# A decoder layer on one core: the last two groups' Toeplitz convolutions as fp32r products of high and low parts

## What is computed

```python
kv = vr[:, :, :, None, :] * x2r[:, :, None, :, :]
k_f = jnp.fft.rfft(k.astype(jnp.float32), n=fft_size)
y = jnp.fft.irfft(jnp.fft.rfft(kv, n=fft_size) * k_f[None, :, None, None, :], n=fft_size)[..., :L]
y = y + kv * skip
out = jnp.einsum('bhijl,bhil->bhjl', y, x1r)
```

## Time and profile before

| | |
|---|---|
| median of three runs | 573.58 us |
| the profiled execution | 574.25 us, span 572.5 us |
| TensorE (PE) | busy 531.6 us, 93% |
| VectorE (DVE) | busy 381.1 us, 67% |
| ScalarE (ACT) | busy 156.8 us, 27% |
| GpSimd (POOL) | busy 132.2 us, 23% |
| DMA | 26.80 MB, mean 47 GB/s |
| granted TensorE clock, mean | 0.97 |

### The profile page before, as it was taken

How to read it: one execution, slowest core, us unless ns; L and a number is a source line. 1 busy time by engine, 2 the same in 40 slices (tenths; PEclk the granted TensorE clock), 3 DMA queues, 4 the chain that set the end, 5 groups by cost and what they waited for, 6 DMA issues and landing times.

```text
span 572.5 us, 8538 instructions
## 1 busy us (share of the span) xinstructions
PE 531.6 (93%) x3152; PEld 426.0 (74%) x3152; DVE 381.1 (67%) x814; ACT 156.8 (27%) x291; POOL 132.2 (23%) x195
## 2 busy tenths in 40 slices
PE   5975699799999999999999999999999999899994
PEld 5734587646887888765888888765888888688883
DVE  4597589877689976875455666875455677823234
ACT  3433101443323222242222112152222111223330
POOL 2020384110005433121004333121004451200001
PEclk9996699989999999999999999999999999999998
DMA  7423231311114110032001110031002110000001
GB/s 204 126 52 82 74 92 56 97 46 26 37 38 131 43 40 9 1 96 91 1 0 60 37 43 10 0 95 55 1 1 56 47 48 0 32 6 2 1 0 37
DMA packets 25257, 26.80 MB, mean 47 GB/s; under 512 B 2816, under 2 KB 22784, under 8 KB 25216
## 3 DMA queue, kind: packets, MB, share of 16 engines
q1 hardware_dynamic: 14208, 15.73, 9.5%
q10 hardware_dynamic: 10576, 8.95, 5.2%
q0 software_dynamic: 432, 1.57, 0.8%
HBM read 24.15 MB, written 2.10 MB: 46 GB/s over the span
## 4 chain that ended last, share of the span: by engine, by line
PE 79%; DVE 12%; issue 3%; ACT 2%; POOL 1%; DMA 1%; ACTq 0%; POOLq 0%; DVEq 0%
PE bank L955 18%; PE bank L957 17%; PE bank L956 17%; PE bank L1002 5%; PE bank L1065 5%; PE bank L1068 5%; PE bank L1066 5%; PE bank L1042 3%; PE bank L1012 2%; DVE qbd L707 2%; DVE weight L664 1%; PE bank L1076 1%; DMA wo_sb<-in_woT 1%; PE bank L1024 1%; DVE ffn_lo L671 1%
## 5 line engine op out<-in xcount | busy, mean ns | idle before, releaser
L955 PE MATMUL bank<-x2T_lo,ffn_hi 128*128 128x512 f32 x256 | 110.9, 433 | 5.0 <-DVE x2T_lo L833 2.9
L906 DVE TENSOR_TENSOR inter<-bank,inter 128x512 f32<-128x512 f32 x64 | 44.2, 690 | 99.7 <-PE bank L957 99.7
L957 PE MATMUL bank<-x2T_hi,ffn_hi 128*128 128x512 f32 x256 | 102.0, 398 | 0.0
L956 PE MATMUL bank<-x2T_hi,ffn_lo 128*128 128x512 f32 x256 | 101.4, 396 | 0.0
L446 POOL TENSOR_TENSOR qbd<-qT_sb,ctxT_sb 128x256 f32<-128x256 f32 x128 | 79.8, 647 | 85.0 <-PE bank L1068 68.7
L955 PE MATMUL bank<-ffn_lo,inter_hi 128*128 128x256 f32 x256 | 77.8, 304 | 1.3 <-DVE inter_lo L900 1.0
L396 POOL TENSOR_TENSOR ve<-ve,minus_half 128x2 f32<-128x2 f32 x24 | 16.8, 716 | 266.7 <-DVE ve L757 198.3
L605 ACT ACTIVATE inter_hi<-inter 128x512 fp32r<-128x512 f32 x64 | 40.4, 632 | 129.4 <-DVE inter L906 129.4
L957 PE MATMUL bank<-ffn_hi,inter_hi 128*128 128x256 f32 x256 | 72.5, 283 | 0.0
L956 PE MATMUL bank<-ffn_hi,inter_lo 128*128 128x256 f32 x256 | 72.4, 283 | 0.0
L599 ACT ACTIVATE inter<-bank 128x512 f32<-128x512 f32 x64 | 38.1, 595 | 124.9 <-PE bank L957 124.9
(11 more groups left out here) (118 smaller groups left out, 793.8 us busy)
## 6 DMA issues: line engine op xcount, KB each, us to landing
toep_sb<-in_toep ACTq DMA_DIRECT2D x64, 128.0 KB, 2.1
xT_sb<-in_xT SPq DMA_DIRECT2D x4, 512.0 KB, 5.4
ctxT_sb<-in_ctxT SPq DMA_DIRECT2D x4, 512.0 KB, 4.7
x_sb<-in_x SPq DMA_DIRECT2D x4, 512.0 KB, 5.8
ctx_sb<-in_ctx SPq DMA_DIRECT2D x4, 512.0 KB, 6.5
out<-ctxT_sb POOLq DMA_DIRECT2D x3, 512.0 KB, 3.4
raw_w<-in_gate_p SPq DMA_DIRECT2D x8, 128.0 KB, 2.3
raw_s<-in_gate_s SPq DMA_DIRECT2D x8, 128.0 KB
```

The costliest lines, as they stand in the source:

```text
L906: nc.vector.tensor_tensor(inter[:, n % 2, :], up_ps[:, :], inter[:, n % 2, :], ALU.mult).then_inc(inter_ready, 1)
L955: nc.tensor.matmul(ps, w_hi, x_lo, start=start, stop=False, skip_group_check=True)
L956: nc.tensor.matmul(ps, w_lo, x_hi, start=False, stop=False, skip_group_check=True)
L957: return nc.tensor.matmul(ps, w_hi, x_hi, start=False, stop=stop, skip_group_check=True)
```

## The change

Groups 2 and 3 (SPLIT_FROM = 2) get another convolution; groups 0 and 1 keep theirs.

- Ahead of group 0 the 16 filters' 383 padded taps are loaded (two small DMAs), rounded to fp32r on ScalarE (taps_hi), and the rest is formed on VectorE (in place). At group 0's norm stage both are stored to DRAM; beside every second convolution of group 1 two DMAs inside DRAM expand two heads' taps into full 128x256 Toeplitz tiles, high and low.
- In groups 2 and 3 ScalarE loads two tiles per head (high and low, 128 KB each) into one of three buffers, two heads ahead.
- kv is split as well: kv_hi on ScalarE, then kv_lo on VectorE, one convolution ahead; GpSimd's products(h) wait for kv_lo(h - 2) instead of the convolution.
- TensorE does two `split_mm`: the diagonal block over all 512 columns, the off-diagonal block over 256.
- The unpacking's buffers are given up to the new tiles.

```diff
+        with ExitStack() as unpacking:
+            def sbu(name, shape, dt=F32):
+                return unpacking.enter_context(nc.sbuf_tensor(name, shape, dt))
+            raw_w = sbu("raw_w", [P, NRAW, QC], I32)
+            raw_s = sbu("raw_s", [P, NSC, QC])
+            weight = sbu("weight", [P, NSC, 2, QC])
+
+        kv_split = sb("kv_split", [P, 2, 2, T], F32R)
+        toep_split = sb("toep_split", [P, NSPLIT, 2, 2 * P], F32R)
...
@@ gpsimd, products
-                if h >= 2:
+                if h >= 2 and g >= SPLIT_FROM:
+                    pool.wait_ge(kvlo_ready, split_count(g, h - 2))
+                elif h >= 2:
                     count(pool, y_mm, 16, g, h - 1)
...
@@ scalar
+            act.dma_start(taps_sb[:, 0:P - 1], toep[:, P - 1, 0:P - 1]).then_inc(ld_taps, 16)
+            act.dma_start(taps_sb[:, P - 1:PADDED], toep[:, 0, :]).then_inc(ld_taps, 16)
...
+            act.wait_ge(ld_taps, 32)
+            nc.scalar.activation(taps_hi, taps_sb, ACT.Copy).then_inc(tapshi_ready, 1)
...
+                if g >= SPLIT_FROM:
+                    kv_hi(g, 0)
+
+            def load_split(g, h):
+
+                if h < NSPLIT - 1:
+                    count(act, y_mm, 16, g, 0)
+                else:
+                    count(act, y_mm, 16, g, h - NSPLIT + 1)
+                for part, taps in enumerate(full):
+                    act.dma_start(toep_split[:, h % NSPLIT, part, :].bitcast(F32), taps.ap()[h]).then_inc(ld_split[h % NSPLIT], 16)
+
+            def kv_hi(g, h):
+
+                act.wait_ge(kv_ready, 32 * g + 2 * h + 2)
+                count(act, y_mm, 16, g, max(h - 1, 0))
+                nc.scalar.activation(kv_split[:, h % 2, 0, :], kv_sb[:, h % 2, :], ACT.Copy).then_inc(kvhi_ready, 1)
...
             def conv(g, h):
 
-                if h + NTOEP - 1 < CH:
+                if g >= SPLIT_FROM:
+                    if h + NSPLIT - 1 < CH:
+                        load_split(g, h + NSPLIT - 1)
+                    if h + 1 < CH:
+                        kv_hi(g, h + 1)
+                elif h + NTOEP - 1 < CH:
                     load_filter(g, h + NTOEP - 1)
+                if g == SPLIT_FROM - 1 and h % 2 == 0:
+                    act.wait_ge(taps_stored, 32)
+                    for taps, rows in zip(compact, full):
+                        two = bass.AP(taps, h * PADDED + P - 1, [[PADDED, 2], [-1, P], [1, 2 * P]])
+                        act.dma_start(rows.ap()[h:h + 2], two).then_inc(full_stored, 16)
 
             def norm(g, _):
-                for h in range(NTOEP - 1):
-                    load_filter(g, h)
+                if g == 0:
+                    act.wait_ge(tapslo_ready, 1)
+                    for part, taps in zip(compact, (taps_hi.bitcast(F32), taps_sb)):
+                        act.dma_start(part.ap(), taps).then_inc(taps_stored, 16)
+                if g == SPLIT_FROM:
+                    act.wait_ge(full_stored, 16 * CH)
+                    act.wait_ge(wlo_ready, NU)
+                if g >= SPLIT_FROM:
+                    for h in range(NSPLIT - 1):
+                        load_split(g, h)
+                else:
+                    for h in range(NTOEP - 1):
+                        load_filter(g, h)
...
@@ vector
+            dve.wait_ge(tapshi_ready, 1)
+            nc.vector.tensor_tensor(taps_sb.bitcast(F32R), taps_sb, taps_hi.bitcast(F32), ALU.subtract)\
+                .then_inc(tapslo_ready, 1)
...
+            def kv_lo(g, h):
+
+                dve.wait_ge(kvhi_ready, split_count(g, h))
+                nc.vector.tensor_tensor(kv_split[:, h % 2, 1, :], kv_sb[:, h % 2, :],
+                                        kv_split[:, h % 2, 0, :].bitcast(F32), ALU.subtract).then_inc(kvlo_ready, 1)
+
+            def x1T(g, _):
+                if g >= SPLIT_FROM:
+                    kv_lo(g, 0)
+
             def conv(g, h):
 
                 if h:
                     conv_sum(g, h - 1)
+                if g >= SPLIT_FROM and h + 1 < CH:
+                    kv_lo(g, h + 1)
...
+                    if prev == 0:
+                        dve.wait_ge(taps_stored, 32)
                     normalise(prev, 1, x_sb, x2_sb)
...
@@ tensor
+            def conv_split(g, h):
+
+                pe.wait_ge(ld_split[h % NSPLIT], 32 * split_loads(g, h))
+                pe.wait_ge(kvlo_ready, split_count(g, h))
+                if h >= 2:
+                    count(pe, z_ready, 16, g, h - 1)
+                n = NB * CI * CI
+                hi, lo = toep_split[:, h % NSPLIT, 0], toep_split[:, h % NSPLIT, 1]
+                kv_hi, kv_lo = kv_split[:, h % 2, 0], kv_split[:, h % 2, 1]
+                split_mm(fb[h % 2][:, :], hi[:, 0:P], lo[:, 0:P], kv_hi, kv_lo, True, False)
+                split_mm(fb[h % 2][:, n:2 * n], hi[:, P:2 * P], lo[:, P:2 * P], kv_hi[:, 0:n], kv_lo[:, 0:n],
+                         False, True).then_inc(y_mm, 1)
```

More of the change, by code:

```diff
@@ L35 @@
 NSC = 4
+NSPLIT = 3
+SPLIT_FROM = 2
+PADDED = 3 * P - 1
 NIBBLE = (1 << 31) | (7 << 22)
@@ L55, in decoder_layer @@
                   gate_p, gate_s, up_p, up_s, down_p, down_s, out):
+    compact = [nc.dram_tensor(name, (CH, PADDED), F32) for name in ("taps_hi_dram", "taps_lo_dram")]
+    full = [nc.dram_tensor(name, (CH, P, 2 * P), F32) for name in ("toep_hi_dram", "toep_lo_dram")]
     x_v = x.rearrange("b t f -> t b f")
@@ L132, in side_ps @@
             return fb[0:2] if g == G - 1 else psum[4:6]
+        taps_sb = x2_sb[0:CH].rearrange("p b f -> p (b f)")[:, 0:PADDED]
+        taps_hi = x2_sb[0:CH].rearrange("p b f -> p (b f)")[:, 2 * D:2 * D + PADDED].bitcast(F32R)
         def second_of(g):
@@ L150, in decoder_layer @@
         ld_toep = sems(*[f"ld_toep{i}" for i in range(NTOEP)])
+        ld_split = sems(*[f"ld_split{i}" for i in range(NSPLIT)])
+        ld_taps, tapshi_ready, tapslo_ready, taps_stored, full_stored, kvhi_ready, kvlo_ready = sems(
+            "ld_taps", "tapshi_ready", "tapslo_ready", "taps_stored", "full_stored", "kvhi_ready", "kvlo_ready")
         fold_mm, proj_mm, v_mm, s_mm, o_mm, ms_mm, rT_mm, wo_mm, x1T_mm = sems(
@@ L181, in decoder_layer @@
         rstd_ready = sems("rstd_ready1", "rstd_ready2", "rstd_ready3")
-        raw_w = sb("raw_w", [P, NRAW, QC], I32)
-        raw_s = sb("raw_s", [P, NSC, QC])
-        weight = sb("weight", [P, NSC, 2, QC])
+        with ExitStack() as unpacking:
[6 more added lines that the diff above has]
+        toep_split = sb("toep_split", [P, NSPLIT, 2, 2 * P], F32R)
+        sb("unpack_rest", [P, QC])
         x2T_hi = sb("x2T_hi", [P, 2, T], F32R)
@@ L287, in schedule, with split_count, split_loads @@
             finish()
+        def split_count(g, h):
+            return CH * (g - SPLIT_FROM) + h + 1
+        def split_loads(g, h):
+            turn_size = len(range(h % NSPLIT, CH, NSPLIT))
+            return turn_size * (g - SPLIT_FROM) + h // NSPLIT + 1
         def spread_waits(eng, g, v):
@@ L933, in _ @@
             schedule(dve, turn, {"score": score, "rms": rms, "factor": factor, "outproj": outproj, "norm": norm,
-                                 "conv": conv}, nothing, inner, split, unpack, last_turn, finish)
+                                 "x1T": x1T, "conv": conv}, nothing, inner, split, unpack, last_turn, finish)
         @block.tensor
@@ L1054, in x1T @@
                             last.then_inc(x1T_mm, 1)
+            def conv_split(g, h):
[9 more added lines that the diff above has]
+                         False, True).then_inc(y_mm, 1)
             def conv(g, h):
+                if g >= SPLIT_FROM:
+                    conv_split(g, h)
+                    return
                 count(pe, ld_toep[h % NTOEP], 16 * CH // NTOEP, g, 16 * (h // NTOEP + 1))
```

## The result

| | before | after |
|---|---|---|
| median | 573.74 us | 616.06 us (4 runs, 611.68 to 616.7) |
| the profiled execution | 574.25 us, span 572.5 | 616.29 us, span 614.6 |
| TensorE busy | 531.6 us | 539.6 us |
| granted clock, mean | 0.97 | 0.954 |

What follows compares the result with a forecast made beforehand. TensorE, busy 93% of the span, was taken to bound the kernel. Group 2's -1.3, group 3's +2.3 and +0.1 ahead of group 0 made +1.1 us on the profiled 574.25, or 574.7 us against the median; range 572.9 to 576.

Steps and rivals of the forecast that it cites:

- TensorE's 1.06 us per convolution: Groups 2 and 3: a split convolution takes 1.06 us on TensorE instead of 1.30, 0.24 less each.
- A' to B': Next slot's convolution after gate to its convolution after up: one convolution of 1.06 us plus up's 1.40.
- Rival (c): Split convolutions: fp32r products spaced like fp32's, so no gain in slots of two; 577.6 us, chance 0.05.
- The slot of three: Stage with three convolutions, walked instruction by instruction: 8.27 us instead of 8.13, no gain, since TensorE waits for kv_lo.
- kv_hi's delay: ScalarE, two filter-load issues ahead of kv_hi: it starts 0.75 us behind inner_hi's or gelu's start; possible 0 to 0.87.
- Rival (a): Slots of three: the gain comes through, slots 0.86 us shorter, 4.3 us over five; 570.4 us, chance 0.25.
- The slot of two: Stage with two convolutions, 10 to 15 of group 2: 6.35 us instead of 6.83, gain 0.48, kv_lo just in time.
- The order on the shared ports: VectorE beside GpSimd: inter_lo starts 0.08 us ahead of GpSimd's products, so it costs 0.60 us, not 1.03.
- Rival (b): VectorE beside GpSimd: GpSimd's products get in ahead of inter_lo, +3.9 us; 578.6 us, chance 0.18.
- Start of the convolutions: Slot 8 of groups 2 and 3: the walk, a step-by-step timing, had conv(0) 1.1 us late, conv(2) 1.0.
- Group 2: Sum over its convolutions: late start +1.1, five slots of two -2.4, conv(15)'s own gain lost; -1.3 us.
- Group 3: Sum: start +1.1, slots 11 to 13 +0.4, last handover +0.5, skip product +0.5, last convolution -0.24; +2.3 us.

Runs made afterwards that it cites:

- e3: The changed kernel with the same sixteen copies inside DRAM issued from SP's queue instead of ScalarE's: 577.83 us, ratio 1.0064 to the kernel before.
- g1: e3 with only convolutions 4 to 15 of group 2 split and kv_hi ahead of the filter loads: 572.0 us, ratio 0.9949 to the kernel before.
- f1: e3 with kv_hi of the next convolution ahead of the two filter loads in ScalarE's stream: 572.6 us, ratio 0.9968 to the kernel before.
- g2: g1 with the expansion in two copies of all 16 heads from SP's queue: 572.07 us, ratio 0.9965 to the kernel before.

## Why the prediction was wrong

**The step that failed** is the sentence "In group 1 the 16 copies inside DRAM of 256 KB: two issues behind every second convolution, in ScalarE's long wait between inner_hi and gelu ..., and 4 MB over some 40 us on queues that are mostly idle: 0, up to +1 if a filter load has to stand behind them". It measured +37.2. Three things in it were taken for granted. The rate: I let 4 MB pass in 40 us on the strength of queues that were mostly idle, while such a copy keeps two engines of 16 busy, so 4 MB need 85 us (16 x 5.3). The issue: I put it at nothing, as if it were the 0.34 to 0.43 us of an issue into an empty queue, and two of every four were about 5 us. The cover: an idle ScalarE hides an issue only if the issue ends before the next instruction of that queue is due. No row of the kernel before has a copy inside DRAM, so the step should have been bounded from both sides like the others. The rule on the number of engines in the Trainium skill's page "DMA: Bandwidth & Descriptors" would have given the two engines, and with them an upper end. That an issue holds its engine for about as long as a copy lasts was shown only by the runs. A fourth thing was missing from the sum, the clock that falls after a stop: most of 12.5 of the 37.2 us. The upper end would have been 16 x 5 us less what group 1's idle ScalarE covers, far outside the range that I gave. The changed kernel's windows show how long the copies really ran: behind the last issue, which ended at 263.55, for another 10 us, close to two copies' length.

```profile
270.00:274.00 4.00, 4.00 (x23) 3.39 (x22) 2.38 (x5) 0.69 (x1) 0.00 (x0) 1.00 0.12 44
274.00:276.00 2.00, 2.00 (x10) 1.60 (x9) 1.70 (x3) 0.69 (x1) 0.00 (x0) 1.00 0.00 0
```

No rival held this either: all three concerned groups 2 and 3.

Point by point for the rest, which e3 shows free of the copies:

- **TensorE's 1.06 us per convolution: right.** A' to B' of 2.52 less up's 1.40 is 1.12, with handovers in it; in g1's slots of two the same distance is 2.45, which leaves 1.05, and the slot is 6.31 against 6.35. Rival (c), fp32r as slow as fp32, fell.
- **The slot of three: right in mechanism, 0.15 short.** 8.40 to 8.42 against 8.27, of which kv_hi's delay, 0.92 instead of 0.75, is 0.17. Rival (a), the gain coming through, needed a slot of 7.4; it fell. f1 confirmed the other end of the same term at 8.08.
- **The slot of two: 0.15 short.** 6.50 against 6.35; the copy "just in time" was 0.17 too late, for the same reason. In f1, where it comes earlier, the slot is 6.31.
- **The order on the shared ports: right.** inter_lo's median in the whole execution is 0.69 us and its longest 0.80, before 1.11. Rival (b) fell.
- **Start of the convolutions: right up to conv(2).** Reckoned from x1T, conv(0) comes 1.12 late (4.81 against 3.69; walk +1.1) behind a kv_lo(0) that took 1.02 us beside GpSimd, and conv(2) 1.15 (10.23 against 9.08; walk +1.0). conv(3) is 2.04 late in group 2 (13.83 against 11.79), where the walk had about 1.5.
- **Group 2: +0.8 instead of -1.3.** conv(15) still starts 0.78 later than before. conv(5) was 1.76 late where the walk had 1.1, the slots of two gave 0.32 each and not 0.48, and one handover more was late: conv(9) starts 3.23 behind conv(8) and not 2.57. Ahead of it the second filter load's issue took 1.11 us instead of 0.45 (rows below), and kv_hi waited for it. In e3 that handover was on time, and group 2 took +0.04.
- **Group 3: +2.9 instead of +2.3, and partly by luck.** Too low was the same term, 0.15 in each slot of three, and one issue of 0.77 (0.33 late). The skip product cost about what was forecast: conv(14) came 3.10 behind conv(13), 0.58 more than without it (forecast +0.5). But the +0.5 for the last convolution never came. conv(15) starts 2.59 behind conv(14), not 3.23, because no filter load is left to be issued ahead of its kv_hi, which started 0.53 behind inner_hi's start.
- **The start: open.** +0.1 was forecast, 0 to 1.9 measured with the taps alone; the subtraction took 0.54 us there, not 0.45.

The issues of the second filter load in the changed kernel (min/median/max in ns):

```profile
L605 ACTq DMA_DIRECT2D toep_split<-toep_lo_dram x32: 449/451/1112, 340.0 to 513.4; - x32
```

Such a long issue, of 0.5 to 1.5 us, came up one to three times in every kernel with these loads, at changing places; what makes it long no run shows.

So the term of the slots that decided was the delay of kv_hi by issues. It was sized 0.17 too low in its usual case and had no allowance for long issues. With the copies out of the way the forecast of +1.1 us stands against +3.2 to +3.7 in e3: outside the range of that sum as well, though by 1 us and not by 40.

What was not tried: copies of one head each, or loading the Toeplitz rows straight from the compact taps into the tiles.

## What to carry to other kernels

A DMA issue is not free because its engine is idle: ask how long the transfer ahead of it in the same queue lasts, and which compute instruction stands behind it. Here the long copies cost nothing in the queue of an engine that computes nothing (e3, g1, g2). If they have to stand in another queue, an outermost dimension of 8 or 16 cut the loss from 37.2 to 9.5 and 12.2 us. And add the clock to the bill: a stop of TensorE is paid again afterwards. And where an fp32 product is replaced by split fp32r ones, the gain is only there while the engines that make the parts have slack in the slot: here it was there with two convolutions in a slot and gone with three.

## What the runs showed of the hardware

- A copy inside DRAM of 256 KB with an outermost dimension of 2 ran at 49 GB/s with a DMA share of 0.14; copies with 8 or 16 there ran at 193 and 326 GB/s at shares of 0.54 and 1.01.
- With one such copy running, ScalarE's queue took the next at 0.60 us. The second copy of a pair and the 128 KB filter load behind it took 4.3 to 5.4 us to issue, and the traffic went on for 10 us behind the last issue. On SP, where the copies came without a gap, all but the first took 4.5 to 7.0 us.
- After a stop of 4.7 us TensorE's granted clock was 0.50 from 195 to 199 us. Over group 1's stretch the mean was 0.88, and the same work kept TensorE busy for 12.5 us more than before, beside the waits.
- With two DMA issues between two activations of ScalarE the second starts 0.92 us behind the start of the first; with the issues behind it instead, 0.54 us.
- VectorE's subtraction of 128x512 took 0.69 us when it started ahead of GpSimd's pair and 1.11 us when it started behind it; GpSimd's pair took 1.59 instead of 1.21 us when it was the later one.
